# Two-layer graph kernel on one core: the remaining f32 products written as three products of f16 halves, with the steps that use them moved by one to three slots

## What is computed

```python
# layer 0
mask = (adj > 0); deg = sum(mask, axis=1)
agg  = mask @ x / max(deg, 1)
l0   = relu(concat([x @ W_self + b_self, agg @ W_nb + b_nb]) @ W_comb + b_comb)
x1   = layernorm(x + l0)
# layer 1
neib_att = tanh(neigh @ Wn1 + bn1) @ Wn2 + bn2      # 4096 x 32
value    = neigh @ Wv + bv                          # 4096 x 128
x_att    = tanh(x1 @ Wx1 + bx1) @ Wx2 + bx2         # 4096 x 32
ws = leaky_relu(x_att @ neib_att.T, 0.01)           # 4096 x 4096
ws = softmax(where(adj > 0, ws, -9e15), axis=1)
out = layernorm(x1 + concat([x1 @ Wfx + bfx, ws @ value]))
```

## Time and profile before

| what | value |
|---|---|
| median of 3 runs | 858.24 us (857.29 to 858.50) |
| the profiled execution, its time | 860.72 us |
| span of its trace | 858.9 us |
| busy share: PE, DVE, ACT, POOL | 90%, 71%, 61%, 40% |
| busy share of PE's weight loads | 73% |
| mean granted TensorE clock | 0.98 |

### The profile page before, as it was taken

One profiled execution on the slowest core, in us unless ns is written; L12 is line 12 of the kernel. 1 busy time (PEld: TensorE's weight loads), 2 busy tenths in 40 slices (PEclk: granted clock), 3 DMA queues, 4 the chain that ended last, 5 costly groups with the idle time before them and its releaser, 6 DMA issues.

```text
span 858.9 us, 18086 instructions
## 1 busy us (share of the span) xinstructions
PE 770.8 (90%) x6416; PEld 630.2 (73%) x6416; DVE 612.5 (71%) x1538; ACT 526.2 (61%) x970; POOL 345.7 (40%) x364
## 2 busy tenths in 40 slices
PE   2996697899999999999999999999999999999885
PEld 2652475787888888888878788788788888878664
DVE  2777845677777777777777777777777777776784
ACT  1234224666766666667666666676666666666794
POOL 0000545344444444444444444444444444444311
PEclk9998798999999999999999999999999999999999
DMA  9800996566666666656566665676656655541000
GB/s 292 286 2 0 202 282 155 136 149 151 160 154 145 150 156 153 141 151 152 140 148 151 161 147 148 149 161 154 146 150 154 157 139 151 151 112 32 7 14 13
DMA packets 175098, 120.28 MB, mean 140 GB/s; under 512 B 140320, under 2 KB 158624, under 8 KB 175008
## 3 DMA queue, kind: packets, MB, share of 16 engines
q1 hardware_dynamic: 171856, 117.63, 54.8%
q10 hardware_dynamic: 3152, 1.49, 0.6%
HBM read 81.34 MB, written 4.19 MB: 100 GB/s over the span
## 4 chain that ended last, share of the span: by engine, by line
PE 45%; DVE 20%; POOL 13%; issue 11%; ACT 6%; ACTq 2%; DMA 1%; POOLq 0%; DVEq 0%
PE ps_agg L893 6%; PE ps_t L859 5%; PE ps_agg L838 5%; PE ps_agg L835 5%; PE ps_v L872 5%; POOL x L343 5%; PE ps_s L850 4%; DVE late L565 4%; POOL bias L362 3%; ACT score L691 3%; DVE score L519 3%; DVE mask L434 3%; PE ps_v L875 3%; PE ps_x L913 3%; PE ps_x L910 2%
## 5 line engine op out<-in xcount | busy, mean ns | idle before, releaser
L691 ACT ACTIVATE score<-ps_s,sc 128x512 f32<-128x512 f32 x256 | 177.2, 692 | 151.5 <-PE ps_s L850 151.5
L835 PE MATMUL ps_agg<-x,mask_t 128*128 128x257 f16 x1024 | 243.6, 276 | 9.9 <-DMA mask_t<-mask 9.9
L565 DVE TENSOR_TENSOR late<-ps_t,late 128x512 f16<-128x512 f32 x256 | 174.4, 681 | 106.5 <-ACT late L704 106.5
L838 PE MATMUL ps_agg<-x,mask_t 128*128 128x256 f16 x1024 | 238.5, 276 | 1.7 <-DMA mask_t<-mask 1.6
L519 DVE CUSTOM_DVE_ANT_0 score<-score,bias 128x512 f32<-128x512 f32 x256 | 181.5, 709 | 73.6 <-ACT score L691 73.4
L872 PE MATMUL ps_v<-v,late 128*128 128x256 f16 x1024 | 198.5, 273 | 3.9 <-DVE late L586 2.5
L362 POOL TENSOR_SCALAR bias<-mask 128x1024 bf16<-128x1024 bf16 x128 | 148.9, 1163 | 94.7 <-DVE part_max L519 66.7
L875 PE MATMUL ps_v<-v,late 128*128 128x128 f16 x1024 | 179.7, 219 | 5.3 <-DVE late L565 5.0
L704 ACT CAST late<-ps_t 128x512 f16<-128x512 f32 x256 | 149.8, 585 | 39.5 <-PE ps_t L859 39.4
L859 PE MATMUL ps_t<-ident,score 128*128 128x128 f32 x1024 | 154.6, 274 | 1.7 <-ACT score L698 1.7
L698 ACT ACTIVATE score<-score,exp_bias 128x1024 f32<-128x1024 f32 x128 | 147.0, 1149 | 0.8 <-DVE exp_bias L528 0.7
(11 more groups left out here) (113 smaller groups left out, 796.5 us busy)
## 6 DMA issues: line engine op xcount, KB each, us to landing
adj_sb<-in_adj_dram SPq DMA_DIRECT2D x128, 512.0 KB, 4.3
neigh_sb<-in_L_gnn_neigh_dram SPq DMA_DIRECT2D x8, 512.0 KB, 10.2
score<-in_x_dram SPq DMA_DIRECT2D x8, 512.0 KB, 9.6
x_in<-in_x_dram SPq DMA_DIRECT2D x32, 128.0 KB, 4.2
out_dram<-out_sb SPq DMA_DIRECT2D x32, 128.0 KB, 4.1
mask_t<-mask SPq DMA_TRANSPOSE x128, 3.1
bias<-in_L_gnn_W_comb_dram ACTq DMA_DIRECT2D x1, 512.0 KB, 7.6
bias<-in_L_gnn_W_self_dram ACTq DMA_DIRECT2D x1, 256.0 KB, 3.7
```

The lines of the kernel that those rows point to most:

```text
L565: dve.tensor_tensor(p_lo[:, k % 2, :], ps_t[k % 2][:, :], p_hi[:, k % 2, :], ALU.subtract).then_inc(p_lo_made, 1)
L691: act.activation(score[:, b % 2, k * GW:(k + 1) * GW], ps_s[k % 2][:, :], ACT.Prelu, alpha=SLOPE, scale=score_scale).then_inc(leaky_made, 1)
L835: mm = pe.matmul(agg[:, 0:D + 1], mask_t[:, c, :], x16[:, c, 0:D + 1], start=(c == 0), stop=(c == NC - 1), skip_group_check=True)
L838: mm = pe.matmul(agg[:, 0:D], mask_t[:, c, :], x16[:, c, X_LO:X_LO + D], start=False, stop=False, skip_group_check=True)
```

## The change

1. Each remaining product of f32 becomes three products of f16: high by high, high by low, low by high. `combine` has 12 products of 256 columns in place of 4, `hidden_and_fx` 12 of 128 columns in place of 4, `x_attention` and the attention of `neigh` one product each, for which three copies (high, high, low) of the 32 hidden rows stand one under another as 96 rows. In the opening `neigh_values` has 24 products per turn in place of 8 and `neigh_hidden` 6 in place of 2.
2. So ACT writes high halves in place of its copies and makes each tanh twice (f32 and f16), and DVE makes the low halves: `mean_low` (512 columns), `x1_low` (256 columns), `tanh_low` (32 rows), and in the opening `rows_low` and `hidden_low`.
3. The table of slots is stretched, which gives each new pair of halves a slot of its own ahead of the product; the last step goes from 38 to 41.
4. The opening: small loads are merged and reordered (18 issued by ACT in place of 23); the folding of the weights stands first on PE; the scale of `neigh` is needed before its first transposed rows are copied; five of the eight low halves of `x` are made by POOL, in two instructions each; the first mask is made during the last four turns.

The diff, cut to its core:

```diff
-MASK_AT = -5
-BIAS_AT = -1
+X_DVE = 3
+X_ORDER = (3, 0, 4, 1, 5, 2, 6, 7)
+MASK_AT = -4
+BIAS_AT = 1
 MEAN_AT = 8
-MEAN_T_AT = 9
-MEAN_COPY_AT = 10
-COMBINE_AT = 11
-LAYER0_AT = 12
-X1_T_AT = 15
-HIDDEN_AT = 16
-XATT_AT = 17
-STACK_AT = 18
-SCORE_AT = 19
-ROW_MAX_AT = 27
-TURN_AT = 29
-WEIGH_AT = 30
-LAYER1_AT = 38
+MEAN_T_AT = 10
+MEAN_SPLIT_AT = 11
+COMBINE_AT = 12
+LAYER0_AT = 13
+X1_T_AT = 16
+X1_SPLIT_AT = 17
+HIDDEN_AT = 18
+TANH_AT = 19
+XATT_AT = 20
+STACK_AT = 21
+SCORE_AT = 22
+ROW_MAX_AT = 30
+TURN_AT = 32
+WEIGH_AT = 33
+LAYER1_AT = 41
...
+            pool.wait_ge(biases_in, 16 * len(BIASES))
+            for c in range(2 * DC):
+                pool.tensor_scalar(b_wide[:, c, :], ident[:, :], 0.0, b_cols[:, c:c + 1],
+                                   ALU.mult, ALU.add).then_inc(b_wide_made, 1)
+            pool.wait_ge(bound_made, 8)
+            pool.partition_all_reduce(sc[:, 0:8], sc[:, 0:8], P, RMAX).then_inc(bound_reduced, 1)
...
+            def x_low(i):
+                pool.wait_ge(x_hi_made, X_ORDER.index(i) + 1)
+                pool.tensor_scalar(x_sb[:, part, :], x_sb[:, part, :], x_scale, None,
+                                   ALU.mult).then_inc(x_sb_scaled, 1)
+                pool.wait_ge(x_sb_scaled, i - X_DVE + 1)
+                pool.tensor_tensor(x16[:, part, X_LO:X_LO + D], x_sb[:, part, :], x16[:, part, 0:D],
+                                   ALU.subtract).then_inc(x_lo_pool, 1)
+            pool.wait_ge(x_scaled, 1)
+            for i in range(X_DVE, NT):
+                x_low(i)
...
+            def mean_low(b):
+                dve.wait_ge(mean_hi_made, b + 1)
+                dve.scalar_tensor_tensor(out=mean_x_t[:, 1, :], in0=ps_agg[b % 2][:, :], scalar=x_scale,
+                                         in1=mean_x_t[:, 0, :], op0=ALU.mult, op1=ALU.subtract).then_inc(mean_lo_made, 1)
...
             def x_tanh(b):
                 act.wait_ge(hf_done, b + 1)
-                act.activation(tanh_sb[:, :], ps_x[0:H, 2 * P:3 * P], ACT.Tanh,
-                               bias=bx1_sb[:, 0:1]).then_inc(tanh_made, 1)
+                for out in (tanh32, tanh16):
+                    act.activation(out[:, :], ps_x[0:H3, 2 * P:3 * P], ACT.Tanh, bias=bx1_sb[0:H3, 0:1],
+                                   scale=h1_inv[0:H3, :]).then_inc(tanh_made, 1)
...
             def combine(b):
-                pe.wait_ge(mean_x_t_copied, b + 1)
-                for c in range(2 * DC):
+                pe.wait_ge(mean_lo_made, b + 1)
+                for k, ((r, w), c) in enumerate(product(HI_LO, range(2 * DC))):
                     half, dc = divmod(c, DC)
-                    mm = pe.matmul(ps_agg[b % 2][:, 0:D], mean_x_t[:, c * P:(c + 1) * P],
-                                   m_both[:, dc, half * D:(half + 1) * D], start=(c == 0), stop=(c == 2 * DC - 1))
+                    mm = pe.matmul(agg[:, 0:D], mean_x_t[:, r, c * P:(c + 1) * P], m16[:, dc, half, w, :],
+                                   start=(k == 0), stop=(k == 6 * DC - 1))
```

More of the change, by code:

```diff
@@ L1 @@
 from contextlib import ExitStack
+from itertools import product
 import concourse.bass as bass
@@ new lines, in split_thrice @@
+            def split_thrice(out, raw, scale):
+                for c in range(DC):
+                    wide = out[:, c].rearrange("p v (k h) -> p v k h", k=3)
+                    thrice = raw[:, c, :].unsqueeze(1).broadcast_to((P, 3, H))
+                    scale_link(dve.tensor_scalar(wide[:, 0], thrice, scale, None, ALU.mult))
+                    last = dve.scalar_tensor_tensor(out=wide[:, 1], in0=thrice, scalar=scale, in1=wide[:, 0],
+                                                    op0=ALU.mult, op1=ALU.subtract)
+                return last
@@ new lines, in stack_second @@
+            def stack_second(out, scaled, raw, scale):
+                wide = out[:, :].rearrange("p (k h) -> p k h", k=4)
+                scale_link(dve.tensor_scalar(scaled, raw[0:H3, :], scale, None, ALU.mult))
+                scale_link(dve.tensor_copy(wide, scaled.unsqueeze(1).broadcast_to((H3, 4, H))))
+                part = slice(H, 2 * H)
+                return dve.tensor_tensor(wide[part], scaled[part].unsqueeze(1).broadcast_to((H, 4, H)), wide[part],
+                                         ALU.subtract)
@@ new lines, in rows_low, with hidden_low @@
+            def rows_low(turn):
+                for dc in range(DC):
+                    dve.wait_ge(rows_hi_made, DC * turn + dc + 1)
+                    dve.scalar_tensor_tensor(out=rows_t[:, turn % 2, dc, 1, :], in0=ps_t[dc][:, :], scalar=n_scale,
+                                             in1=rows_t[:, turn % 2, dc, 0, :], op0=ALU.mult,
+                                             op1=ALU.subtract).then_inc(rows_lo_made, 1)
+            def hidden_low(turn):
+                dve.wait_ge(h_tanh, 2 * turn + 2)
+                part = slice(2 * H, H3)
+                dve.tensor_tensor(h_t16[part, :], h_t32[part, :], h_t16[part, :], ALU.subtract).then_inc(h_split, 1)
@@ L599, in _ @@
                     masked_scores(*d)
+                if d := due(s, MEAN_SPLIT_AT, 0):
+                    mean_low(d[0])
+                if d := due(s, X1_SPLIT_AT, 0):
+                    x1_low(d[0])
+                if d := due(s, TANH_AT, 0):
+                    tanh_low(d[0])
                 if d := due(s, LAYER1_AT - 1, 0):
@@ L815, in _ @@
                     neigh_attention(turn - 1)
-                if turn == 1:
-                    combine_weights()
             neigh_attention(NT - 1)
```

510 lines of the change are left out of this document (283 added, 227 removed).

## The result

The changed kernel takes **880.98 us** (median of 4 runs, 877.94 to 882.22) beside 858.37 of the kernel before (4 runs, 857.29 to 861.93): a ratio of 1.025, 95% interval 1.0225 to 1.0271. It is slower by 22.6 us. The forecast of 816 us, its range and its sign were wrong. The profiled execution took 882.22 us, with a span of 880.4.

What follows compares the result with a forecast made beforehand. PE was taken to bound the kernel: 28 blocks at −1.74 us give −49, opening +4, depth +3, so a span of 858.9 becomes 817, forecast as a median of 816 us. Range 798 to 838.

Steps and rivals of the forecast that it cites:

- Term 1: PE's wait ahead of `hidden_and_fx` for ACT's copy of the transposed x1 goes: −0.96 us per block.
- Term 2: `combine` on PE, as twelve f16 products, takes 1.32 us in place of 1.73: −0.41 per block.
- Term 3: `hidden_and_fx` on PE, twelve narrow f16 products at 0.07, takes 0.85 us in place of 1.10: −0.25 per block.
- Term 4: `x_attention` on PE becomes one narrow f16 product, 0.09 us in place of 0.51: −0.42 per block.
- Term 5: New low halves add 1.4 us per block to DVE (16.8 to 18.2), a tanh 0.3 to ACT, covered by PE.
- Term 6: PE waits for ACT's exponentials at the turn in slot 2, behind DVE's `degrees` and the mean: +0.3 us per block.
- Rival D: DVE's waits for ACT, 5.6 us per block, don't shrink: period 23.8, 890 us; chance 0.04.
- Opening: Start up to block 1: DVE bounds, then POOL's halves of x; block 1 at 111 or 112: +4 us, −6 to +18.
- Rival C: POOL and DVE hold each other up in the opening, for a total time of 831 us; chance 0.12.
- Depth: The last step comes 3 slots later, which lengthens the tail: +3 us, between 0 and +6.

Runs made afterwards that it cites:

- experiment 9: Kernel before, with only ACT's copy of the transposed x1 moved ahead of the mean: 826.84 us, ratio 0.9614.
- experiment 6: Changed kernel with masks, bias, mean, `add_fx` and both tanh reordered, `b_wide` on DVE: 806.9 us; with all low halves of x on DVE too, 798.49 us.
- experiment 2: Changed kernel with the five low halves of x that POOL makes given to DVE: 871.33 us.
- experiment 3: Changed kernel with POOL making the bias of the first three blocks only: 861.17 us, period 22.15.
- experiments 6 and 7: The reordered kernel at 798.49 us, then one order edit taken back at a time: mean 828.02, masks 811.75, bias 793.19, `add_fx` 798.78 us.

## Why the prediction was wrong

- **Term 1** (−0.96): right in size, and it came. It was the order in ACT's queue alone (experiment 9).
- **Term 2** (1.32 for `combine`): right, 1.31.
- **Term 3** (0.85 for `hidden_and_fx`): 0.67, the low bound of 0.055 per product, for a run of twelve. The estimate from the Trainium skill (TensorE: Matmul & The Clock Gate, section Back-to-back issue gap), 0.97, doesn't hold here; weight loads of 96 and 128 columns stay hidden beside them.
- **Term 4** (0.09): 0.06, right.
- **Term 5** (DVE +1.4, covered): the durations were about right: `mean_low` has a mean of 746 ns and `x1_low` of 419. The cover was not there. DVE is busy 19.15 of 22, which for the period of 22.64 makes 19.7, and the forecast was 18.2. Of the 1.5 between them, 0.5 is `masked_scores` (eight rows, in the repeating part 771 ns for 706) and 0.7 the masks (four rows, 869 ns for 687), both long beside POOL. The rest is small: `tanh_low` takes 0.33, not 0.25, two rows of `layer0` and `add_fx` got 0.06 longer each, and the base was 17.0, not 16.8.
- **Term 6** (+0.3) is the step that failed. "What is late next" was asked of one reader of ACT's slot, the exponentials. `layer1` was counted as taken out of the stretch, −1.35, and the text didn't ask who waits for it where it stands now. It is still due in the slot of the product that needs its tile free, but now stands behind `degrees` and a mask. DVE's stretch up to `degrees` was mis-sized too, 9.63 for 8.35, for its `masked_scores` and a mask were long beside POOL. In place of 0.3 PE waits 0.53 + 0.80 + 0.32 in rows, 2.25 per block as distances between starts (22.64 less the 20.39 of the run in which PE has no gap). The 0.32, though of the forecast size and for L817, is not the wait that was forecast: it stands in slot 4, not 2, and comes of the two tanh ahead of the exponentials (experiment 6). The runs show it from both sides: the two edits that shorten the way from `degrees` to `layer1` bring 1.34 together, and each taken back brings PE's wait for that tile back.
- **Rival D** named the sign and the queue, and its sign came: a period above 22 with PE waiting for L674. Its mechanism, fixed waits of DVE, was wrong: DVE waits less than before (L674 for ACT 44.0 us in the run, was 106.5), and PE waits for DVE.
- **Opening** (+4, to +18 at the worst): +27.1. The +4 was counted from 107.81; from the true start of block 1, 104.15, the forecast of 111 or 112 is +7 or +8. This is the second step that failed. The first high half came at 46.6, not at 33: the reduction on POOL was known to stand behind `b_wide`, but the 7.59 us ahead of it has no row in the trace of before, where no such pair occurs, and no term in the prediction. The phase of the turns took 68 us in place of 61. POOL's price for a piece of x was forecast at 5.0 and is 4.9; its last piece ended at 125.7, not at 103, since the first began at 92.67, not at 78, and POOL stood idle another 7.4 us between pieces for ACT's high halves of x.
- **Rival C**: its sign came (block 1 after 120), but its mechanism was small where it was priced: about 3 of the 10 us of DVE (experiment 2). It was right in kind: the rule of the Trainium skill (SBUF — State Buffer, section Who interferes with whom) is borne out by rows, a `masked_scores` of 0.88 to 0.92 in place of 0.68 beside POOL. The masks were lengthened too (1.15 in place of 0.69), though they have one SBUF input. For these the same section names a second case that the prediction had not drawn on: a `tensor_scalar` between SBUF tiles that runs in a two-port mode takes the shared port as well; 1024 columns in 0.68 us, beside 0.68 for 512 columns of two operands, agree with such a mode, which no run here tests. And it acted in the repeating part as well, where the prediction had no term for it: without POOL's bias the period is 0.48 shorter (experiment 3).
- **Depth** (+3): +6.1 from block 30 to the end.

Of the forecast −49 + 4 + 3, the run gave −6.6 + 22 + 6 (the opening as it stands at the `combine` of block 4). With the order mended (experiments 6 and 7) the same products give a period of 20.64, and 20.39 at best, below the 21.15 forecast: the terms on the products were sound, the order around them was not. Against the kernel before with its two lines moved (21.85, experiment 9), the new products at their best are worth 1.46 per block; terms 2 to 4 had said 1.08.

## What to carry to other kernels

When a table of slots is stretched, list for every moved step both what it waits for and who waits for what it frees; a buffer's reader that lands right behind a wait of another queue costs as much as a late producer. Look first for a wait that a change of order in one queue removes: here two lines were worth 3.9%, and the whole change, in the order that it came with, made the kernel 2.5% slower. Where two waits end ahead of the same instruction, test the edits together, and take them back one by one, since singly each shows only the other wait.

## What the runs showed of the hardware

- A `partition_all_reduce` on POOL behind `tensor_scalar` rows started 7.59 us after them with nothing to wait for, and a `tensor_scalar` behind a reduction 7.09 us after it, 1.45 us after its input. Where POOL had waited 20.18 us for its input, the reduction started at once (21.90).
- POOL takes 2.84 us for a product of 128x1024 f32 with a column scalar and 2.06 us for the subtraction of two operands of that size; DVE does both in one instruction of 1.28 us, and five of them in 6.07.
- f16 products of 128 columns, each with its own weights, follow each other every 0.055 us in a run of twelve.
- DVE's mask (one int32 operand of SBUF, 128x1024) takes 0.68 alone and up to 1.53 beside POOL's bias or `norm1`.
